# All tiles of a five-engine kernel written out with constant waits, in a new order, with more spare products in its drain

## What is computed

```
# 1: cross attention with 16 heads of 16 over 257 context rows of each sample
x = rmsnorm(layernorm(x)); q = x @ wq.T; k = ctx @ wk.T; v = ctx @ wv.T
out = softmax(q k / 4, masked) v @ wo.T;  x1 = x_in + sigmoid(x @ wg.T) * out
# 2: causal self attention, 16 query heads and 4 key heads, ternary weights, rotary embedding
# 3: feed-forward layer, 704 wide, ternary weights, activations rounded to 8 bits
z = quant(xn) @ w1.T; h = silu(z) * (quant(xn) @ w3.T); y = x2 + quant(h) @ w2.T
```

## Time and profile before

| | us |
|---|---|
| median of 3 runs | 587.21 (586.63 to 587.69) |
| the profiled execution, its own time | 588.98 |
| its span, first to last instruction | 586.8 |
| mean granted TensorE clock | 0.988 of full |

### The profile page before, as it was taken

The page is one execution under the profiler, slowest core; times in us unless marked ns, Lnnn a source line. Parts: engine busy times, 40 slices in busy tenths (PEclk is TensorE's granted clock), DMA queues, the critical chain, the costliest instruction groups (busy, mean ns, idle before and its releaser), DMA issues. The chain is left out here.

```text
span 586.8 us, 22549 instructions
## 1 busy us (share of the span) xinstructions
PE 542.5 (92%) x7142; PEld 451.6 (77%) x7142; DVE 447.2 (76%) x1389; ACT 424.1 (72%) x1208; POOL 325.0 (55%) x490
## 2 busy tenths in 40 slices
...
## 3 DMA queue, kind: packets, MB, share of 16 engines
...
...
## 5 line engine op out<-in xcount | busy, mean ns | idle before, releaser
L894 ACT ACTIVATE pr<-sm,nb 128x257 f32<-128x257 f32 x256 | 129.0, 507 | 8.9 <-DVE nb L1133 7.5
L678 POOL TENSOR_TENSOR cTl<-cx,cTh 128x516 fp32r<-128x516 f32 x64 | 86.1, 1345 | 74.7 <-ACT cTh L790 74.5
L1133 DVE CUSTOM_DVE_ANT_0 sm<-x_ps,mbias 128x257 f32<-128x257 f32 x256 | 99.8, 421 | 28.4 <-PE x_ps L1440 24.7
L790 ACT ACTIVATE pt<-x_ps 128x512 f32<-128x512 f32 x112 | 64.9, 594 | 10.3 <-PE x_ps L1450 6.9
L1450 PE MATMUL x_ps<-tab,pr 128*128 128x128 f32 x512 | 71.5, 274 | 0.7 <-DVE o L1164 0.4
L790 ACT ACTIVATE kk<-x_ps 128x257 f32<-128x257 f32 x128 | 49.2, 387 | 29.2 <-PE x_ps L1331 29.1
L1450 PEld LDWEIGHTS x_ps<-tab,pr 128*128 128x128 f32 x512 | 57.2, 141 | 4.3 <-issue 1.7
L1331 PE MATMUL x_ps<-cTh,wkTh 128*128 128x258 f32 x256 | 60.2, 317 | 0.3 <-ACT pt L790 0.2
L687 POOL TENSOR_TENSOR sr<-sv,halfneg 128x20 f32<-128x20 f32 x16 | 56.7, 3543 | 1.3
L1331 PE MATMUL x_ps<-wvTh,cTh 128*128 128x256 f32 x256 | 56.8, 303 | 0.1
L1440 PE MATMUL x_ps<-kk,qbd 32*64 32x257 f32 x1024 | 44.7, 404 | 10.7 <-POOL qbd L699 5.7
...
## 6 DMA issues: line engine op xcount, KB each, us to landing
...
```

The lines of the kernel that those rows point to most:

```text
L678: g.tensor_tensor(cxbuf(cT[1], b)[:, :, :], cx[:, b % BT, :, :], cxbuf(cT[0], b)[:, :, :].bitcast(F32), ALU.subtract).then_inc(A_ctl, 1)
L790: return sc.activation(dst, src, ACT.Copy)
L894: sc.activation(pr[:, b % 2, gr, :], sm[:, b % 2, gr, :], ACT.Exp, bias=nb[:, n:n + 1], scale=-1.0, accum_out=st[:, 0, b, gr:gr + 1]).then ...
L1133: v.tensor_tensor_reduce(out=sm[:, b % 2, gr, :], in0=xb(f"S{b}", gr)[:, 0:LK], in1=mbias[:, b, :], scale=1.0, scalar=0.1 * NEG, op0=ALU.a ...
```

## The change

- `run` emits the list "each" once for every round from 3 to 13 with a constant i. The loop and `apart` are gone, and all waits compare with constants.
- The lists of all five engines are in another order, in each of the three parts; the steps are the same.
- The table BANK gives many products other banks.
- SPARE has 19 entries instead of 13, 256 products in all instead of 167.

Core of the diff (the parts "first" and "last" are left out, and all but one of the removed lines with `apart`):

```diff
--- before.py
+++ after.py
@@ -56,13 +56,13 @@
 
 
 BANK = {
-    "K10": (2,), "K11": (1,), "V1": (4,), "K20": (6,), "K21": (1,), "V2": (2,), "K30": (1,), "K31": (3,), "V3":
+    "K10": (3,), "K11": (5,), "V1": (4,), "K20": (6,), "K21": (5,), "V2": (2,), "K30": (4,), "K31": (1,), "V3":
     (2,), "K40": (5,), "K41": (4,), "V4": (0,), "B_O": (5,), "B_oT": (4,), "B_wo": (4,), "B_xT": (5,), "B_qkv":
-    (5,), "D_QT": (1,), "D_kT": (0,), "D_S": (1,), "D_PV": (5,), "D_yT": (6,), "D_pj": (0,), "C_xT": (2,), "C_z0":
-    (6,), "C_z1": (2,), "C_z2": (0,), "C_hT": (2,), "C_y": (1,), "GATE": (6,), "Q_h": (5,), "Q_q": (3,), "PT00":
-    (3,), "PT01": (6,), "PT10": (4,), "PT11": (4,), "PT20": (0,), "PT21": (4,), "PT30": (2,), "PT31": (1,), "FS0":
-    (3,), "TT0": (6,), "TT1": (3,), "TT2": (0,), "TT3": (1,), "FS1": (1,), "FS2": (6,), "B_st": (3,), "S0": (5, 3,
-    4, 6,), "S1": (3, 2, 5, 0,), "S2": (3, 2, 5, 0,), "S3": (0, 4, 3, 1,), "P_h": (0,), "P_q": (1,), "P_k0": (2,),
+    (5,), "D_QT": (1,), "D_kT": (3,), "D_S": (1,), "D_PV": (6,), "D_yT": (3,), "D_pj": (3,), "C_xT": (6,), "C_z0":
+    (6,), "C_z1": (2,), "C_z2": (0,), "C_hT": (5,), "C_y": (5,), "GATE": (6,), "Q_h": (5,), "Q_q": (6,), "PT00":
+    (2,), "PT01": (6,), "PT10": (3,), "PT11": (0,), "PT20": (0,), "PT21": (1,), "PT30": (5,), "PT31": (2,), "FS0":
+    (2,), "TT0": (5,), "TT1": (3,), "TT2": (6,), "TT3": (1,), "FS1": (6,), "FS2": (4,), "B_st": (0,), "S0": (2, 4,
+    6, 1,), "S1": (5, 2, 3, 0,), "S2": (2, 3, 5, 0,), "S3": (0, 1, 3, 4,), "P_h": (0,), "P_q": (1,), "P_k0": (2,),
     "P_k1": (3,), "P_v": (4,), "P_vx": (5,),
...
     "pe": {
...
         "each": [
-            ("S", 0), ("K", 1, 0), ("K", 1, 1), ("C_xT",), ("B_st",), ("D_kT",), ("V", 1), ("B_O",), ("D_QT",),
-            ("PT", 0, 0), ("PT", 0, 1), ("D_S",), ("S", 1), ("B_oT",), ("K", 2, 0), ("K", 2, 1), ("B_wo",),
+            ("S", 0), ("B_st",), ("K", 1, 0), ("K", 1, 1), ("V", 1), ("C_xT",), ("D_kT",), ("B_O",), ("D_QT",),
+            ("PT", 0, 0), ("PT", 0, 1), ("D_S",), ("S", 1), ("K", 2, 0), ("B_oT",), ("K", 2, 1), ("B_wo",),
             ("S", 2), ("PV", 0), ("C_z", 0), ("V", 2), ("PT", 1, 0), ("K", 3, 0), ("B_xT",), ("PT", 1, 1),
-            ("K", 3, 1), ("B_qkv",), ("C_z", 1), ("S", 3), ("GATE",), ("Q_h",), ("C_z", 2), ("PV", 1), ("D_PV",),
-            ("V", 3), ("Q_q",), ("PT", 2, 0), ("PT", 2, 1), ("D_yT",), ("C_hT",), ("K", 4, 0), ("K", 4, 1),
-            ("C_y",), ("D_pj",), ("PT", 3, 0), ("PT", 3, 1), ("PV", 2), ("V", 4), ("PV", 3),
+            ("C_z", 1), ("K", 3, 1), ("B_qkv",), ("S", 3), ("GATE",), ("C_z", 2), ("Q_h",), ("V", 3), ("D_PV",),
+            ("PV", 1), ("K", 4, 0), ("PT", 2, 0), ("D_yT",), ("Q_q",), ("C_hT",), ("PT", 2, 1), ("D_pj",), ("C_y",),
+            ("PV", 2), ("PT", 3, 0), ("K", 4, 1), ("PT", 3, 1), ("V", 4), ("PV", 3),
         ],
...
     "act": {
...
         "each": [
-            ("CT", 2), ("K", 1, 0), ("EXP", 0, 0), ("EXP", 0, 1), ("EXP", 0, 2), ("K", 1, 1), ("EXP", 0, 3),
-            ("C_xT",), ("D_QT",), ("PT", 0, 0), ("V", 1), ("CT", 3), ("PT", 0, 1), ("B_oT",), ("K", 2, 0),
-            ("K", 2, 1), ("EXP", 1, 0), ("D_S",), ("EXP", 1, 1), ("EXP", 1, 2), ("EXP", 1, 3), ("V", 2),
-            ("PT", 1, 0), ("EXP", 2, 0), ("B_xT",), ("C_z", 0), ("K", 3, 0), ("PT", 1, 1), ("K", 3, 1), ("CT", 4),
-            ("EXP", 2, 1), ("B_qkv",), ("C_z", 1), ("Q_h",), ("C_z", 2), ("EXP", 2, 2), ("EXP", 2, 3), ("GATE",),
-            ("EXP", 3, 0), ("EXP", 3, 1), ("D_PV",), ("V", 3), ("PT", 2, 0), ("EXP", 3, 2), ("EXP", 3, 3),
-            ("C_hT",), ("D_yT",), ("CT", 5), ("K", 4, 0), ("B_keep",), ("PT", 3, 0), ("PT", 3, 1), ("Q_q",),
-            ("K", 4, 1), ("V", 4),
+            ("CT", 2), ("K", 1, 0), ("EXP", 0, 0), ("K", 1, 1), ("EXP", 0, 1), ("EXP", 0, 2), ("EXP", 0, 3),
+            ("C_xT",), ("D_QT",), ("PT", 0, 0), ("V", 1), ("PT", 0, 1), ("EXP", 1, 0), ("B_oT",), ("K", 2, 0),
+            ("K", 2, 1), ("CT", 3), ("EXP", 1, 1), ("EXP", 1, 2), ("EXP", 1, 3), ("C_z", 0), ("EXP", 2, 0),
+            ("EXP", 2, 1), ("D_S",), ("PT", 1, 0), ("V", 2), ("CT", 4), ("K", 3, 0), ("B_xT",), ("C_z", 1),
+            ("PT", 1, 1), ("K", 3, 1), ("B_qkv",), ("EXP", 2, 2), ("EXP", 2, 3), ("C_z", 2), ("EXP", 3, 0),
+            ("Q_h",), ("GATE",), ("EXP", 3, 1), ("EXP", 3, 2), ("D_PV",), ("K", 4, 0), ("PT", 2, 0), ("D_yT",),
+            ("C_hT",), ("Q_q",), ("CT", 5), ("EXP", 3, 3), ("V", 3), ("PT", 3, 0), ("B_keep",), ("K", 4, 1),
+            ("PT", 3, 1), ("V", 4),
         ],
...
     "dve": {
...
         "each": [
-            ("S", 0, 0), ("S", 0, 1), ("S", 0, 2), ("D_scale",), ("B_comb",), ("B_den",), ("B_comb2",), ("S", 0, 3),
-            ("D_kT",), ("B_o1",), ("B_O",), ("B_fin",), ("D_S",), ("S", 1, 0), ("S", 1, 1), ("S", 1, 2),
-            ("S", 1, 3), ("D_mx",), ("Q_stats",), ("D_s3",), ("S", 2, 0), ("S", 2, 1), ("B_wo",), ("B_x1",),
-            ("S", 2, 2), ("D_dn",), ("B_norm",), ("Q_norm",), ("B_xT",), ("C_z", 0), ("C_h", 0), ("S", 2, 3),
-            ("D_p3",), ("D_p4",), ("S", 3, 0), ("B_qkv",), ("S", 3, 1), ("C_z", 1), ("C_h", 1), ("S", 3, 2),
-            ("C_z", 2), ("C_h", 2), ("C_q", 0), ("C_q", 1), ("C_q", 2), ("S", 3, 3), ("PT", 2, 1), ("D_yT",),
+            ("B_comb",), ("S", 0, 0), ("S", 0, 1), ("S", 0, 2), ("Q_stats",), ("B_den",), ("D_scale",),
+            ("B_comb2",), ("S", 0, 3), ("B_o1",), ("D_kT",), ("B_O",), ("B_fin",), ("D_S",), ("S", 1, 0), ("D_mx",),
+            ("S", 1, 1), ("S", 1, 2), ("S", 1, 3), ("D_s3",), ("B_wo",), ("S", 2, 0), ("B_x1",), ("S", 2, 1),
+            ("S", 2, 2), ("S", 2, 3), ("C_z", 0), ("C_h", 0), ("B_norm",), ("D_dn",), ("B_xT",), ("C_z", 1),
+            ("D_p3",), ("C_h", 1), ("S", 3, 0), ("B_qkv",), ("Q_norm",), ("D_p4",), ("S", 3, 1), ("C_z", 2),
+            ("S", 3, 2), ("C_h", 2), ("C_q", 0), ("S", 3, 3), ("C_q", 1), ("C_q", 2), ("D_yT",), ("PT", 2, 1),
             ("C_y",), ("D_pj",), ("D_xstats",), ("D_xq", 0), ("D_xq", 1), ("D_xq", 2),
         ],
...
     "pool": {
...
         "each": [
-            ("PX", 0), ("CL", 2), ("CL", 3), ("D_vbd",), ("Q_root",), ("B_root",), ("PX", 1), ("CL", 4),
-            ("B_qkroot",), ("PX", 2), ("B_rope",), ("PX", 3), ("D_yroot",), ("CL", 5), ("D_xroot",), ("QBD", 0),
-            ("QBD", 1), ("EX",), ("QBD", 2), ("QBD", 3),
+            ("Q_root",), ("D_vbd",), ("CL", 2), ("PX", 0), ("PX", 1), ("CL", 3), ("B_root",), ("CL", 4),
+            ("B_qkroot",), ("D_yroot",), ("QBD", 0), ("QBD", 1), ("CL", 5), ("D_xroot",), ("PX", 2), ("PX", 3),
+            ("QBD", 2), ("QBD", 3), ("EX",), ("B_rope",),
         ],
...
     "sp": {
...
         "each": [
-            ("LX",), ("LMB", 0), ("LCTX", 0), ("LMB", 1), ("LCTX", 1), ("LCTX", 2), ("LMB", 2), ("LMB", 3),
-            ("LVX",), ("B_shuffle",), ("LCTX", 3), ("LXR",), ("C_store",),
+            ("LX",), ("LCTX", 0), ("LCTX", 1), ("B_shuffle",), ("LVX",), ("LMB", 0), ("LCTX", 2), ("LMB", 1),
+            ("LMB", 2), ("LCTX", 3), ("LXR",), ("C_store",), ("LMB", 3),
         ],
...
@@ -311,9 +312,10 @@
 
 EARLY = 25
 SPARE = {
-    (16, "B_xT", 0): 20, (16, "B_qkv", 0): 5, (16, "D_PV", 0): 4, (16, "D_yT", 0): 2, (16, "C_hT", 0): 6,
-    (17, "C_xT", 0): 32, (17, "D_PV", 0): 28, (17, "D_yT", 0): 2, (17, "D_pj", 0): 1,
-    (18, "C_xT", 0): 32, (18, "C_z", 0): 3, (18, "C_hT", 0): 28, (18, "C_y", 0): 4,
+    (16, "B_oT", 0): 6, (16, "B_wo", 0): 3, (16, "B_xT", 0): 9, (16, "B_qkv", 0): 9, (16, "D_PV", 0): 23,
+    (16, "D_yT", 0): 5, (16, "C_hT", 0): 10, (16, "D_pj", 0): 3, (17, "C_xT", 0): 43, (17, "D_kT", 0): 2,
+    (17, "D_S", 0): 2, (17, "D_PV", 0): 37, (17, "D_yT", 0): 5, (17, "C_hT", 0): 10, (17, "C_y", 0): 3,
+    (18, "C_xT", 0): 36, (18, "C_z", 0): 4, (18, "C_hT", 0): 39, (18, "C_y", 0): 7,
 }
...
@@ -549,18 +551,12 @@
 
         block = ctx_stack.enter_context(nc.Block())
 
-        def run(eng, name, body):
+        def run(name, body):
 
             body(listed(name, "first"))
-            body(at_each(name, FIRST))
-            with eng.Fori(FIRST + 1, LAST, 1) as i:
+            for i in range(FIRST, LAST):
                 body(at_each(name, i))
             body(listed(name, "last"))
-
-        def apart(eng, i):
-
-            if not isinstance(i, int):
-                eng.nop(nofuse=True)
 
         def cxbuf(tensor, n):
 
...
                         sp.wait_ge(Q_hn, i + 1)
-                        apart(sp, i)
                         load_x(i + 1, xq, L_xq)
...
@@ -1433,7 +1412,6 @@
                         pe.wait_ge(Q_bd, 4 * i + b + 1)
                         for was_read, n_read in read(f"S{b}"):
                             pe.wait_ge(was_read, n_read)
-                            apart(pe, i)
                         for m in range(2):
                             for r in range(NR):
                                 at = slice(r * RG, (r + 1) * RG)
```

(46 more changed lines are left out.)

175 lines of the change are left out of this document (83 added, 92 removed), and 95 rows, old and new, of the table SCHEDULE.

## The result

The changed kernel takes 577.18 us (median of 5 runs, 575.93 to 578.44) against 587.21 (586.63 to 588.22): 0.9827 of the time, interval 0.9807 to 0.9846, so 10.0 us faster. Forecast were 572.4 and 563 to 581. The profiled execution took 578.44, the longest of the five and 1.3 above the median; its span is 576.6.

The account below looks back on a forecast made before the run. TensorE, busy 92% of the span, was taken to bound the kernel. Gains of 11.6 us (tiles 3 to 13), 1.0 (14 and 15), 0.5 (0 to 2) and 1.7 (drain) made 14.8, giving 572.4 us, range 563 to 581.

Parts of the forecast that it names:

- likeliest case: Whole kernel: loop cost gone, about half of the other waits closed, 567 to 577 us; chance 0.56.
- The loop's cost: Loop tiles against written-out tile 3: 0.70 us a tile, 6.3 us for nine tiles and about 0.3 for tile 13.
- Part 2: New order inside tiles 3 to 13: TensorE's products stay the same, its holes shrink, a tile costs 31.9 us.
- qbd hole: TensorE before S 0, waiting for GpSimd's qbd: 0.58 us a tile, closed by moving Q_q and QBD 0 and 1 earlier.
- the wait for xn before B_xT: TensorE before the transposes of xn, waiting for VectorE: 0.40 us a tile, of which 0.1 to 0.4 is left.
- the order gains nothing: Rival: new holes as large as those closed, only the loop's cost and some of the drain earned, 579 us; chance 0.20.
- The osc hole: TensorE before C_hT: VectorE reaches osc some 0.3 to 0.5 us late in the new order, a new hole.
- B_st: TensorE's B_st, moved directly behind S 0: EX's chain of 4.95 us just fits in 5.0; hole 0, bound 0.5.
- The banks: Several tight bank reuses on TensorE (D_QT, K 2 1, PT 3 0), each ready within 0.2 us; together 0.2 a tile.
- Code fetch: Instruction fetch of written-out tiles: taken as costing nothing; as a rival, holes of 0.7 lose the loop's gain, 579 us, chance 0.03.
- The ends: Hand-written tiles 14 and 15 gain 1.0 us (bounds -1 to 2), tiles 0 to 2 gain 0.5 (-1.5 to 2).
- The drain: End of the kernel: 89 more spare products keep TensorE's clock up, gaining 1.7 us, bounds 3 and -1.

Follow-up runs that it names:

- run 1: Kernel before with the loop and `apart` gone, rounds written out, its old lists, banks and spares kept: 573.88 us, 0.9763.
- run 2: Kernel before with the changed kernel's order, banks and spares, its loop and `apart` kept: 588.37 us, 1.0006.
- run 3: Changed kernel with the old table SPARE, 167 spare products at their old places: 576.99 us, 0.9821.
- runs 9 and 10: Changed kernel, TensorE's B_O put behind D_QT: 577.86 us; the same plus C_y behind PV 2 and K 4 1 ahead of PT 3 0: 586.61.

## Why the prediction was right, and where it was not

The time is within the range, 4.8 us above the forecast and just outside the likeliest case's own 567 to 577. That it came so near is partly luck: two terms were wrong and partly cancel. For tiles 3 to 13 the forecast was 6.6 us by the loop and 5.0 by the order, 11.6 in all. Measured are 12.8 by the loop (run 1) and -6.8 by the order, 6.0 in all.

- **The loop's cost, 0.70 a tile, was mis-sized.** Run 1 measures 1.24 a round for rounds 4 to 13, 12.4 us instead of 6.6. The comparison with tile 3 failed because tile 3 was no loop-free round: written out all the way it takes 31.96 in run 1, not 32.36. TensorE's starts in the two agree within 0.02 up to PV 3, and all of the 0.40 lies between PV 3 and the S 0 of round 4, where the loop is entered. And tile 3 has waits at its start that later rounds don't have: those of run 1 take 31.78.
- **That the order gains (Part 2) had the wrong sign.** 5.0 of the 11.6 us were to come from holes closed. The order costs 0.51 or 0.64 a round. The prediction's own mark for being wrong, a period of 32.4 or more, was met with 32.42. The step that failed is the list of holes that the order was to close: most of them were the loop's. Besides the qbd hole (below), the wait for xn before B_xT falls from 3.9 us in rounds 4 to 13 of the kernel before to 2.1 in run 1, and is 2.0 in the changed kernel. The old order, written out, runs at 31.78, already inside the 31.3 to 31.9 that the prediction took for a tile without holes. What was left for the order to win was small, and it lost more at D_kT and B_O and at D_pj and C_y. The second-ranked rival, "the order gains nothing" (579), was nearer than the forecast, with the loop's larger gain covering the order's loss.
- **The qbd hole** did close, but not by the new order: from PV 3 to S 0 are 0.58 us in the changed kernel and 0.59 in run 1, against 1.23 in the loop before. With the new order in the loop (run 2) it is mostly 1.14. The prediction had read from the earlier trace rows that the loop made part of it, and gave the rest to the order.
- **The osc hole** (0.25 forecast) did not come. **B_st** had no hole, as forecast, and had more room than the 0.05 us that the sum left it: ste is ready 0.70 before it in each round, as EX ends 4.31 us behind C_y and not 4.95. **The banks** (0.2 forecast) cost little in their own order: PT 3 0 starts 0.15 late behind VectorE's yo, which reads the bank's last product.
- **Code fetch** cost nothing that shows, as forecast.
- **The ends:** tiles 0 to 2 gave 1.3 once B_st's new place is taken out (0.5 forecast); as start times there differ by up to 5 us between profiles of the same start, no run shows this gain. Tiles 14 and 15 gave 0.5 (1.0 forecast), but see the shift of GATE; with the drain they gave 2.9 (2.7 forecast).
- **The drain** gave 2.4 (1.7 forecast, bounds 3 and -1), 1.3 of it by the spares in run 3's comparison; the other 1.1 may be no more than the shift of GATE. Clock, D_S and C_y came out at 1.00, 1.13 and 0.81 where 1.00, 1.16 and 0.83 were forecast.

The wait for xn in rounds 4 to 13, of the kernel before and of run 1:

```profile
PE x_ps L1521 <- DVE xn L1202: 3.9, 10, 0.4
```

```profile
PE x_ps L1496 <- DVE xn L1179: 2.1, 8, 0.5
```

What stays open: why the new order's rounds stay above 32.1. The timeline shows where they lose, but runs 9 and 10, which should have won it back, only moved the waits, and no run has the new order with the old banks. The split of the loop's cost into register waits and branch is a difference only. The kernel of run 1, 573.88 us, beats both.
